# First attention: value products in halves of 256 queries between the two scores by key

## What is computed

```python
C_q = x @ Wq_d + bq_d                     # 12 numbers a token
C_kv = x @ Wkv_d + bkv_d                  # 4 numbers a token
q = (C_q @ W_qk + b_qk).reshape(b, s, 32, 4)
scores = jnp.einsum('bqhd,bkd->bhqk', q, C_kv) / 2
attn = jax.nn.softmax(scores, axis=-1)
V = (C_kv @ Wv_u + bv_u).reshape(b, s, 32, 16)
out = jnp.einsum('bhqk,bkhd->bqhd', attn, V).reshape(b, s, 512)
return out @ Wo + bo
```

## Time and profile before

| | us |
|---|---|
| runs before (3) | 2521.23, 2543.26, 2550.11 |
| median | 2543.26 |
| profiled execution, its own time | 2546.09 |
| its span | 2544.4 |
| mean granted TensorE clock | 0.929 |
| first attention's loop, first maxima to last value product | 70.0 to 335.0 |

### The profile page before, as it was taken

One profiled execution on the slowest core, in us unless ns is written; L12 is line 12 of the kernel. 1 busy time (PEld: TensorE's weight loads), 2 busy tenths in 40 slices (PEclk: granted clock), 3 DMA queues, 4 the chain that ended last, 5 costly groups with the idle time before them and its releaser, 6 DMA issues. The chain is left out here.

```text
span 2544.4 us, 33798 instructions
## 1 busy us (share of the span) xinstructions
PE 2254.6 (89%) x11776; PEld 1543.1 (61%) x11776; DVE 1447.4 (57%) x2609; ACT 1121.7 (44%) x2682; POOL 673.7 (26%) x842
## 2 busy tenths in 40 slices
PE   4899997887999999999987699999999977899988
PEld 3333355665777777776765566766666655554455
DVE  4667745416566565656645355555555544757744
ACT  2357743124444444444434355555555533325542
POOL 2000000435344444344330111111211102635400
PEclk9569978988999999999998799999999977989998
DMA  2000003462110111011002000000000001864400
GB/s 80 7 1 1 1 20 133 96 139 73 38 50 30 38 50 38 30 50 38 17 34 69 25 31 15 17 31 31 31 31 20 26 17 45 199 108 69 70 18 34
DMA packets 101216, 117.76 MB, mean 46 GB/s; under 512 B 42213, under 2 KB 56933, under 8 KB 98874
## 3 DMA queue, kind: packets, MB, share of 16 engines
q0 software_dynamic: 60096, 50.89, 9.5%
q1 hardware_dynamic: 40954, 64.72, 7.6%
HBM read 83.97 MB, written 31.46 MB: 45 GB/s over the span
## 5 line engine op out<-in xcount | busy, mean ns | idle before, releaser
L1831 POOL TENSOR_TENSOR attn0b_probs<-attn0b_probs,attn0b_recip 128x128 f32<-128x128 f32 (+3 forms) x256 | 192.5, 773 | 223.3 <-DVE attn0b_recip L2067 223.2
L2452 ACT ACTIVATE attn1a_probs<-attn1a_scores,attn1a_negmax 128x128 f32<-128x128 f32 (+3 forms) x256 | 132.6, 523 | 175.7 <-DVE attn1a_negmax L2570 175.7
L1936 ACT ACTIVATE attn0b_probs<-attn0b_scores,attn0b_negmax 128x128 f32<-128x128 f32 (+3 forms) x256 | 132.6, 523 | 150.0 <-DVE attn0b_negmax L2060 148.9
L1497 DVE TENSOR_REDUCE attn0a_negmax<-attn0a_by_query 128x2 f32<-128x1024 f32 x128 | 151.5, 1220 | 54.3 <-PE attn0a_by_query L1576 54.1
L2221 PE MATMUL attn0b_out<-attn0b_probsT,attn0b_v_now 128*128 128x512 f32 x320 | 153.9, 612 | 11.5 <-DVE attn0b_probsT L2074 11.5
L1944 ACT ACTIVATE attn0b_probsT<-attn0b_turned 128x128 f32<-128x128 f32 (+3 forms) x128 | 56.0, 437 | 243.2 <-PE attn0b_turned L2208 242.8
L2391 POOL TENSOR_TENSOR attn1a_q_tok<-attn1a_part_a,attn1a_part_b 128x256 f32<-128x256 f32 x64 | 47.3, 739 | 349.6 <-DVE attn1a_part_b L2595 349.6
L2570 DVE TENSOR_REDUCE attn1a_negmax<-attn1a_scores 128x2 f32<-128x256 f32 (+3 forms) x128 | 105.6, 825 | 52.5 <-PE attn1a_scores L2770 50.3
L2060 DVE TENSOR_REDUCE attn0b_negmax<-attn0b_scores 128x2 f32<-128x256 f32 (+3 forms) x128 | 104.8, 819 | 47.0 <-PE attn0b_scores L2197 47.0
L2782 PE MATMUL attn1a_turned<-ident_f,attn1a_probs 128*128 128x128 f32 x640 | 114.3, 277 | 17.9 <-DVE attn1a_probsT L2578 16.1
L1588 PE MATMUL attn0a_by_key<-attn0a_shifted,attn0a_keys 32*128 32x512 f32 x256 | 113.3, 584 | 16.2 <-ACT probsT_odd L1444 8.3
(11 more groups left out here) (521 smaller groups left out, 6232.1 us busy)
## 6 DMA issues: line engine op xcount, KB each, us to landing
pre<-in_b_o SPq DMA_DIRECT2D x16, 1024.0 KB, 5.6
pre<-in_b_q SPq DMA_DIRECT2D x8, 1024.0 KB, 6.0
attn1b_k_mix<-attn1b_k_spread POOLq DMA_DIRECT2D x32, 192.0 KB, 3.7
attn1b_q_mix<-attn1b_q_spread POOLq DMA_DIRECT2D x32, 192.0 KB, 4.6
pre<-in_b_kv SPq DMA_DIRECT2D x5, 1024.0 KB, 5.5
attn0b_vals<-attn0b_v_out SPq DMA_DIRECT2D x16, 256.0 KB, 4.5
attn0b_keys_hi<-attn0b_part_hi POOLq DMA_DIRECT2D x32, 128.0 KB, 5.2
attn0b_keys_lo<-attn0b_part_lo POOLq DMA_DIRECT2D x32, 128.0 KB, 7.6
```

The lines of the kernel that those rows point to most:

```text
L1497: dve.tensor_reduce(into, by_query[g % 2][:, :, :], AX.X, ALU.max, negate=True).then_inc(s_max, 1)
L1831: pool.tensor_tensor(x, x, recip[:, r % 2, e:e + 1].broadcast_to([P, (qt + 1) * P]), ALU.mult).then_inc(s_scaled, 1)
L1936: act.activation(probs[:, r % 2, e, 0:width], scores[r % 2][:, e, 0:width], ACT.Exp, bias=negmax[:, r % 2, e:e + 1], accum_out=sums[:, r % ...
L2452: act.activation(probs[:, r % 2, e, 0:width], scores[r % 2][:, e, 0:width], ACT.Exp, bias=negmax[:, r % 2, e:e + 1], accum_out=sums[:, h % ...
```

## The change

`times_v` takes a half: queries 0 to 255 or 256 to 511, so that each of its matmuls streams 256 columns, and a step has 8 calls in place of 4. The bank is cleared by the first matmul of half 0 only. One half stands in every round, between the round's two scores by key, instead of a whole key tile after both in every other round: key tile 0 in rounds 4 and 5, tile 1 in 6 and 7, tile 2 in rounds 0 and 1 of the next pass and tile 3 in 2 and 3. In round 4 the half comes after both scores by key. The counts of `s_pv` double, and ScalarE copies the output in round 3 instead of 2.

```diff
--- before.py
+++ after.py
@@ -1440,12 +1440,12 @@
                 kt, j = divmod(u, G)
                 act.wait_ge(s_by_key, NU * step + u + 1)
                 if u == 0 and step >= 2:
-                    act.wait_ge(s_pv, QT * (step - 1))
+                    act.wait_ge(s_pv, 2 * QT * (step - 1))
                 act.activation(probsT[step % 2][:, kt, j, :, :].rearrange("p t q -> p (t q)"), by_key[u % 2][:, :],
                                ACT.Exp).then_inc(s_exp, 1)
 
             def output(step):
-                act.wait_ge(s_pv, QT * (step + 1))
+                act.wait_ge(s_pv, 2 * QT * (step + 1))
                 if step >= 2:
                     act.wait_ge(s_aux, FILL["T", step - 2])
                 act.activation(o_sb[:, step % 2, :, :], out[:, :, :], ACT.Copy).then_inc(s_osb, 1)
@@ -1459,7 +1459,7 @@
                     if g >= 1 and 1 <= step <= STEPS:
                         exponential(step - 1, 2 * g - 2)
                         exponential(step - 1, 2 * g - 1)
-                    if g == 2 and step >= 2:
+                    if g == 3 and step >= 2:
                         output(step - 2)
                     if g == 3 and step + 1 < STEPS:
                         signed_queries(step + 1)
@@ -1588,16 +1588,17 @@
                 pe.matmul(by_key[u % 2][:, :], keys[rows, bass.ts(b * QT + kt, P)], shifted[rows, step % 2, :],
                           start=True, stop=True).then_inc(s_by_key, 1)
 
-            def times_v(step, kt):
+            def times_v(step, kt, half):
                 turn, b = divmod(step, BATCH)
                 pe.wait_ge(s_exp, NU * step + G * (kt + 1))
-                if kt == 0 and step >= 1:
+                if kt == 0 and half == 0 and step >= 1:
                     pe.wait_ge(s_osb, step)
+                of = slice(2 * half, 2 * half + 2)
                 for j in range(G):
-                    last = pe.matmul(out[2 * HD * j:2 * HD * (j + 1), :, :].rearrange("v t q -> v (t q)"),
+                    last = pe.matmul(out[2 * HD * j:2 * HD * (j + 1), of, :].rearrange("v t q -> v (t q)"),
                                      values[:, b * QT + kt, G * turn + j, :],
-                                     probsT[step % 2][:, kt, j, :, :].rearrange("p t q -> p (t q)"),
-                                     start=kt == 0, stop=kt == QT - 1)
+                                     probsT[step % 2][:, kt, j, of, :].rearrange("p t q -> p (t q)"),
+                                     start=kt == 0 and half == 0, stop=kt == QT - 1 and half == 1)
                 last.then_inc(s_pv, 1)
 
             def back_to_tokens(step):
@@ -1617,16 +1618,20 @@
                         scores(step, g)
                     if g == 0 and step >= 2:
                         scores_by_key(step - 2, NU - 2)
+                    if g >= 1 and 1 <= step <= STEPS:
+                        scores_by_key(step - 1, 2 * g - 2)
+                    if g < 4 and step >= 2:
+                        times_v(step - 2, 2 + g // 2, g % 2)
+                    if g >= 5 and 1 <= step <= STEPS:
+                        times_v(step - 1, (g - 4) // 2, g % 2)
+                    if g == 0 and step >= 2:
                         scores_by_key(step - 2, NU - 1)
                     if g >= 1 and 1 <= step <= STEPS:
-                        scores_by_key(step - 1, 2 * g - 2)
                         scores_by_key(step - 1, 2 * g - 1)
+                    if g == 4 and 1 <= step <= STEPS:
+                        times_v(step - 1, 0, 0)
                     if g == 0 and 1 <= step <= STEPS:
                         turn_maxima(step - 1)
-                    if g in (0, 2) and step >= 2:
-                        times_v(step - 2, 2 + g // 2)
-                    if g in (4, 6) and 1 <= step <= STEPS:
-                        times_v(step - 1, (g - 4) // 2)
                     if g == 2 and step + 1 < STEPS:
                         project_queries(step + 1)
                     if g == 5 and step >= 2:
```

## The result

The changed kernel takes 2642.81 us (median of 4 runs, 2638.17 to 2652.18), against 2543.33 for the kernel before in the same comparison (4 runs, 2521.23 to 2550.11). The ratio is 1.041, with a 95% interval of 1.035 to 1.047: 99 us slower. The profiled execution took 2639.64, its span is 2637.9, against 2544.4 before.

A forecast was written before the change was run, and what follows sets the result against it. TensorE was taken to bound the loop at 1.2 GHz, a three-engine chain at 2.4. Low clock throughout: +0.4 (step 0 to 1), +100.2 (14 steps), +2.5 (tail), together +103: 2649 us profiled, 2647 median; range 2600 to 2675.

The forecast's parts named there:

- The clock: First attention's loop: TensorE stays at 1.2 GHz to the loop's end, chance 76%; 14 steps cost +100.2 us.
- one dense run: Fourth full step: product, scores, transposes, scores, product unbroken before the clock rose; the changed loop has no stretch as dense.
- Rival A: Clock rises at the same place; nearly four steps at +2.1, ten at +0.7: +15, 2560 us; chance 7%.
- The size of a step: Loop step on TensorE: 22.8 us in place of 20.7 at 1.2 GHz, 14.5 against 13.8 at 2.4 GHz.
- the way out of a burst: From scores to another shape on TensorE at 1.2 GHz: 0.72 us, of which 0.29 is emptying.
- Round 3: Round with three projections on one row group, then out and half: 3.2 us at 1.2 GHz.
- the stretch with the shift: Step start: first score by key waits for VectorE's shift, to 1.9 us; with out and half 3.6.
- Step 0 to 1: Loop's start, where only the first four halves exist: 17.0 becomes 17.4 us, +0.4.
- the tail: After the last maxima to the last value products: 19.9 becomes 22.4 us at 1.2 GHz, +2.5.
- the transposes back with round 6: Second score, out, transposes back to tokens 1.05, then round 6's burst, out, half: 3.5 us at 1.2 GHz.
- The copy: ScalarE's output copy one round later: its 1.30 us wait goes; costed at nothing at 1.2 GHz.
- rival B: Clock is full from the loop's first steps: 14 steps at 14.5 us, 2519 us in all; chance 4%.

The follow-up runs named there:

- The kernel with the clock held more: Changed kernel plus twenty zero-weight dense matmuls once at step 1 and seventeen in every later step: 2568.66 us, ratio 1.008.
- the raised kernel: Changed kernel plus twenty zero-weight dense matmuls once, behind the maxima's transposes of step 1: 2633.15 us, ratio 1.038.
- the held one: Changed kernel plus twenty zero-weight dense matmuls once at step 1 and seven in every later step: 2641.93 us, ratio 1.037.
- the kernel before raised: Kernel before plus twenty zero-weight dense matmuls once, behind the maxima's transposes of step 1: 2526.93 us, ratio 0.997.
- raised and held: Kernel before plus twenty zero-weight dense matmuls at step 1 and two in rounds 2 and 4 of every later step: 2526.30 us, ratio 0.999.

## Why the prediction was right, and where it was off

**The clock.** The forecast rested on the clock standing at 1.2 GHz to the end of the loop, and it did, from 59.0 to 441.3 us. Had the changed loop had the clock of before, 3.7 of the 14 steps would be at 1.2 GHz (218.2 is 3.7 of 20.66 and 10.3 of 13.78, about). At +1.70 each (22.36 - 20.66), and +0.48 for the other 10.3 (14.26 - 13.78), that is +11. The other 82 of the 93.6 are the clock. This is an estimate from one step of 14.26; no run had the changed order at the clock of before. The kernel with the clock held more shows it from the other side.

**Why the clock stayed down** was argued only in part. The prediction had the rise missed for want of one dense run. Three runs speak against this as the whole cause: the order with whole products between the scores rose three times and fell after 7 us; the changed kernel lost a clock given to it after 24 us; and with halves in the old place the clock rose at 101.9, where the same order of shapes had not raised it in the kernel before. The step that holds is that the changed order stays at 1.2 GHz, and the runs show it to be so with a rise and without one. The step that fails is that a single dense run decides, and that the place of the rise is a property of the order. By that the forecast had the right clock in part for a wrong reason. Rival A was worth less than its 7%: after the falls at 123.1 in the raised kernel and 136.8 in the held one, ten steps at the high clock behind a rise at 174.6 are unlikely. Its price was nearly right (+15 forecast, +11 by the measured steps, tail aside). What in the order decides stays open: the shapes that follow each other, the same matmuls over 14.26 us in place of 13.78, or something else. No run varied rows, columns and density one at a time, and the seventeen added matmuls that held the clock changed all of them.

**The size of a step** was 22.36 in place of 22.8 at 1.2 GHz, and 14.26 in place of 14.5 at 2.4. The mis-sized term is the way out of a burst. I took 0.72 for every one, from a row where the last score had just opened its row group. Where the last score is itself the second on its row group, 0.59 behind the first, it is 0.55 (146.85 to 147.40). Together these are 1.14, which is the 0.72 of a burst without a second plus its 0.43, so the forecast counted 0.17 twice. By that a burst with its half is 0.59 + 0.55 + 1.01, so 2.15, and not 2.3. Three such bursts a step (rounds 2, 7 and the next 0) give the 0.4. Round 3, 0.19 shorter for the same reason, makes up for the stretch with the shift (0.10 longer) and for some hundredths elsewhere. Thirteen steps of 0.44 less are 5.7 us, and the last step, 21.1 in place of 22.0, gives 0.9: together the 6.6 between +100.2 and +93.6.

The other terms, forecast against measured: a half 1.0 and 1.01, at 2.4 GHz 0.57 and 0.57; transposes to the end of the first half 3.6 and 3.70, with the first score by key at 2.00 in place of 1.9; round 3 with the projections 3.2 and 3.01; round 4 3.2 and 3.21; round 5 1.7 and 1.74; the transposes back with round 6 3.5 and 3.50. The shift is exposed as forecast, of which 0.15 is plain idle time. Step 0 to 1 and the tail cost 0.4 and 0.6 more than laid out, and the rest of the program, which the change does not touch, came out 4.0 shorter; the clock behind the loop took another course in the two executions.

**The copy.** Costed at nothing at 1.2 GHz, and that held (20.66 with it alone). At 2.4 GHz the later copy costs 0.3 to 0.5 a step; that it does so by the chain of copy, signed queries and exponential which the prediction named was not followed in the trace. What the prediction did not foresee is that this goes with a loss of the clock in the old order: 34 us from moving a copy whose own work is 0.60 us a step. For the loss of the changed kernel the later copy is not needed, since the order with whole products and the old copy takes the same time. Halves in the new place with the copy in the old one were not run.

**The rule that speaks against the forecast.** By the page "TensorE: Matmul & The Clock Gate" of the Trainium skill, section "Why this matters for your kernels", a TensorE kept busy gets the full clock, which would have made the changed loop as fast as rival B. The loop of after was busy for 21.9 of 22.3 us and had 1.2 GHz to its end. The measurement decides: in this loop the rule does not hold.

## What to carry to other kernels

Read the granted clock of the stage before anything else, and count how often TensorE goes from one tile shape to another: at 1.2 GHz each way out and back cost 0.3 to 0.45 us here, which is small beside what the clock did with the same reordering. A loop that holds 2.4 GHz in part can hold it for less after a small edit on another engine: here the later copy on ScalarE came with 78.5 us at the high clock in place of 140.5. A run of dense matmuls at the loop's start is a cheap way to see which part of a difference is the clock.

## What the runs showed of the hardware that was not expected

- A busy TensorE is not enough to keep the clock. It fell from 2.4 to 1.2 GHz after stretches busy for 8.31 of 9.30 us and 9.94 of 10.30 us, with no idle time above 0.46 us in the first. Twenty dense bf16 matmuls brought it up each time they were tried, but not at a fixed distance: 0.9 us behind the first in the changed kernel raised (99.2 for a row at 98.26), and 4.9 us in the kernel before raised (102.7 for a row at 97.83).
- The clock can swing in a loop of equal steps: up 6.8 us four times with 10.2 us down in between, with halves in the old place; then 85 us down, and up for 85 us, with nothing changed in the work.
- The kernel before itself spreads over 2.4% from run to run, and the time goes with the mean granted clock: of 21 runs the shortest took 2513.83 at 0.945 and the longest 2573.01 at 0.917. With the clock raised by hand, 11 runs spread over 0.4%, and with it raised and held over 0.7%. So most of this kernel's spread goes with how long the clock is up; that it is so in this loop, and not elsewhere in the program, is read from the smaller spread alone.
- Leaving a burst of 32-row tiles costs 0.29 us at 1.2 GHz behind a score that opened its row group, and 0.12 (0.55 - 0.43) behind one that was the second on it.
